# A gapless opening, and query and key projections in three products of rounded parts for images 3 to 7

## The chip, the core and the metric

The kernel runs on one core of a Trainium2 chip. The core has five engines that run their own instruction streams and meet only at semaphores: TensorE (PE in the rows, with its weight loads as PEld), VectorE (DVE), ScalarE (ACT), GpSimd (POOL) and SyncE (SP), which here issues all transfers. TensorE reads SBUF and writes PSUM; GpSimd works on SBUF alone. The metric is the device time of one launch in microseconds (us).

## What is computed

An attention block on eight images of 32 x 32 pixels with 64 channels, in float32: a group norm (8 groups), projections to queries, keys and values, a softmax over all 1024 pixels, the output projection, and the normalised input added back.

```
xf = group_norm(x, gamma, beta).reshape(B, N, C)      # B=8, N=1024, C=64
q, k, v = xf @ wq + bq, xf @ wk + bk, xf @ wv + bv
attn = softmax(einsum('bnc,bmc->bnm', q, k) * C ** -0.5)
out = einsum('bnm,bmc->bnc', attn, v) @ wp + bp
return xf + out
```

## The kernel before

**Tiles.** An image lies in SBUF twice: turned (`x_T`, channels in the partitions, pixels 0 to 511 in partitions 0 to 63 and 512 to 1023 in partitions 64 to 127) for the projections, and pixel by pixel (`values`) for the weighing and the residual. The scores of an image are made in eight tiles `i` of 128 x 1024, each exponentiated by ScalarE into `probs[i]` (L411); TensorE weighs the values with them (L846), and GpSimd adds the eight tiles up for the denominators (`sum_probs`, L309, seven additions per image).

**Number formats.** Matmuls in float32 are two instructions each in the trace. The scores are made of rounded parts instead: `q_hi`, `q_lo`, `k_hi`, `step_hi`, `step_lo` have the type fp32r, and each matmul with them is one instruction. A value is split by rounding it to fp32r (high part) and subtracting (low part); three products, high x high, high x low and low x high, stand in for the full one (`score_terms`, L788). The projections of queries (`project_q`, L752, two products that use one half of the rows each) and keys (`project_k`, L746, two products that use one half of the columns each) are in float32.

**Blocks.** A block `b` is the work in which the scores of image `b` are exponentiated and weighed. Image `p = b + 1` gets its row maxima in the same block (`max_chunk`, L759: eight chunks, each reduced by VectorE in L582 before the next may overwrite `wide`), image `s = b + 2` is normalised and projected, and image `z = b + 3` has its statistics taken. Normalising is one VectorE instruction (`normalise`, L537); the statistics go TensorE (mean) - ScalarE (squares) - TensorE (variance) - VectorE (`add_eps`, L529) - GpSimd (`rstd_of`, L275) - ScalarE (`gain_of`, L376). The block ends with the projection of image `s`, the transposed maxima, the weighing of tiles 6 and 7 and the output projection (L870). Images 0 and 1 are prepared by hand-written code in the opening. There the first chunks of maxima (L759, L582) follow the projection of image 0, and `keep_warm` (L876) issues products of ones that nobody reads.

**What sets the order.** Each engine's order is written out by hand; only semaphores tie them. In block 0 ScalarE waits for `gain_of(2)` between tiles 4 and 5. GpSimd's order in a block is the seven additions, then `rstd_of(z)`, `split_first(s)` (L291), `split_step(s)` (L296). TensorE's order at a block's end reads:

```
next_max_chunk(p, 7)
pe.wait_ge(xn_done, s - 1)
pe.wait_ge(exp_done, T * b + T)
project_q(s, ...)
project_k(s, ...)
```

## Time and profile before

| | us |
|---|---|
| median of 3 runs (200.02 to 200.08) | 200.05 |
| the profiled execution | 201.43 |
| its span, from first to last instruction | 199.6 |
| TensorE busy in the span | 189.2 |
| GpSimd busy | 143.4 |
| VectorE busy | 136.1 |
| ScalarE busy | 111.2 |

The profiled execution is 1.38 us longer than the median, and 1.83 us of it lie around the span. Times in rows are microseconds from the span's start. TensorE's matmuls are pipelined and overlap in the rows, so the start of one to the start of the next is the honest price.

### The profile page before, as it was taken

The numbers are of one execution on the slowest core, as the hardware profiler recorded it, in microseconds if no ns is written. First come the engines' busy times: TensorE is split into PE (matmuls) and PEld (weight loads), VectorE is DVE, ScalarE is ACT, GpSimd is POOL, SyncE is SP. The second block draws the span as 40 slices with busy tenths as digits, with TensorE's granted clock in tenths as the row PEclk, the third lists the DMA queues.
The fourth block names the chain that finished last, engine by engine and source line by source line (L and its number), as shares of the span: only waits on it lengthen the run. The fifth ranks groups of instructions, "written<-read, shape, count | busy, mean of one in ns | idle before, by whom it ended". The sixth has DMA issues, their size and how long they took to land.

```text
span 199.6 us, 3301 instructions
## 1 busy us (share of the span) xinstructions
PE 189.2 (95%) x1226; PEld 97.3 (49%) x1226; DVE 136.1 (68%) x179; ACT 111.2 (56%) x181; POOL 143.4 (72%) x92
## 2 busy tenths in 40 slices
PE   7895989989999999999999999999999999999993
PEld 7721435533564365536454466436452646444432
DVE  3239656697569786678767685868667856909763
ACT  2519267646865466546863676546544665338611
POOL 4108559599999979999699969996999869970000
PEclk9758599999999999999999999999999999999999
DMA  5594000000000001000100010000100010001002
GB/s 169 197 393 162 0 0 3 0 0 7 0 2 0 3 13 43 3 0 2 56 0 0 2 56 2 0 0 22 36 0 2 5 53 0 0 5 53 0 9 100
DMA packets 4415, 6.95 MB, mean 35 GB/s; under 512 B 832, under 2 KB 1456, under 8 KB 4400
## 3 DMA queue, kind: packets, MB, share of 16 engines
q1 hardware_dynamic: 4400, 6.75, 9.6%
q8 instruction: 10, 0.16, 0.4%
q14 instruction: 5, 0.04, 0.1%
HBM read 4.59 MB, written 2.10 MB: 34 GB/s over the span
## 4 chain that ended last, share of the span: by engine, by line
PE 80%; DVE 5%; DMA 4%; issue 3%; POOL 3%; ACT 2%; SPq 1%; DVEq 0%; POOLq 0%; ACTq 0%
PE attn L846 25%; PE scores L788 24%; PE wide L759 10%; PE scores L752 4%; PE misc L870 3%; PE scores L746 3%; DVE chunk_max L582 3%; POOL prob_sum L309 2%; DMA packed<-in_packed_dram 2%; PE misc L854 2%; PE attn L746 2%; DMA max_rows<-max_T 2%; PE misc L734 1%; ACT probs L411 1%; PE misc L861 1%
## 5 line engine op out<-in xcount | busy, mean ns | idle before, releaser
L309 POOL TENSOR_TENSOR prob_sum<-prob_sum,probs 128x1024 f32<-128x1024 f32 x42 | 102.0, 2428 | 5.7
L582 DVE TENSOR_REDUCE chunk_max<-wide 128x1 f32<-128x1024 f32 x60 | 73.4, 1223 | 31.5 <-PE wide L759 31.0
L411 ACT ACTIVATE probs<-scores 128x1024 f32<-128x1024 f32 x64 | 63.1, 1022 | 29.3 <-PE scores L788 28.5
L846 PE MATMUL attn<-probs,values 128*64 128x512 f32 x256 | 62.0, 605 | 0.0
L759 PE MATMUL wide<-k_hi,q_hi 64*128 64x512 f32 x120 | 31.0, 483 | 1.8 <-DVE chunk_max L582 1.8
L846 PEld LDWEIGHTS attn<-probs,values 128*64 128x64 f32 x256 | 15.6, 136 | 26.5 <-issue 24.1
L309 POOL TENSOR_TENSOR prob_sum<-probs 128x1024 f32<-128x1024 f32 x7 | 16.7, 2380 | 11.8 <-ACT probs L411 11.8
L759 PEld LDWEIGHTS wide<-k_hi,q_hi 64*128 64x128 f32 x120 | 12.5, 185 | 22.9 <-DVE chunk_max L582 13.2
L788 PE MATMUL scores<-q_hi,step_hi 64*128 64x512 f32 x96 | 20.7, 425 | 0.5
L788 PE MATMUL scores<-q_lo,step_hi 64*128 64x512 f32 x96 | 19.2, 391 | 0.0
L788 PE MATMUL scores<-q_hi,step_lo 64*128 64x512 f32 x96 | 19.1, 391 | 0.0
L383 ACT ACTIVATE q_hi<-scores,bias_q 128x512 fp32r<-128x512 f32 x13 | 8.9, 685 | 15.1 <-PE scores L752 15.1
L275 POOL TENSOR_TENSOR rstd<-var_eps,minus_half 128x1 f32<-128x1 f32 x8 | 4.4, 552 | 12.2 <-DVE var_eps L529 12.2
L788 PEld LDWEIGHTS scores<-q_hi,step_hi 64*128 64x128 f32 x96 | 9.2, 185 | 6.8 <-ACT probs L411 3.1
L788 PEld LDWEIGHTS scores<-q_lo,step_hi 64*128 64x128 f32 x96 | 9.2, 184 | 1.9
L599 DVE TENSOR_TENSOR misc<-misc,inv_den 128x512 f32<-128x512 f32 x7 | 4.9, 699 | 7.5 <-PE misc L870 7.5
L788 PEld LDWEIGHTS scores<-q_hi,step_lo 64*128 64x128 f32 x96 | 9.2, 185 | 1.4
L752 PE MATMUL scores<-xn,packed 64*128 64x512 f32 x28 | 8.3, 674 | 0.7 <-DVE xn L537 0.7
L567 DVE SCALAR_TENSOR_TENSOR q_lo<-scores,bias_q,q_hi 128x512 fp32r<-128x512 f32 x12 | 8.8, 729 | 0.0
L870 PEld LDWEIGHTS misc<-w_vp_s,attn_T 128*64 128x64 f32 x112 | 6.5, 137 | 3.8 <-issue 3.8
L296 POOL TENSOR_TENSOR step_lo<-step,step_hi 128x384 fp32r<-128x384 f32 x8 | 8.1, 1016 | 0.0
L620 DVE TENSOR_TENSOR prob_sum<-prob_sum,probs 128x1024 f32<-128x1024 f32 x6 | 7.3, 1218 | 1.1 <-ACT probs L411 0.6
(132 smaller groups left out, 236.7 us busy)
## 6 DMA issues: line engine op xcount, KB each, us to landing
x_T<-in_x_turned_dram SPq DMA_DIRECT2D x8, 256.0 KB, 6.4
values<-in_x_dram SPq DMA_DIRECT2D x8, 256.0 KB, 6.5
out_dram<-y_out SPq DMA_DIRECT2D x7, 256.0 KB, 2.0
out_dram<-y_out SPq DMA_DIRECT2D x2, 128.0 KB, 1.7
max_rows<-max_T SPq DMA_DIRECT2D x14, 4.0 KB
packed<-in_packed_dram SPq DMA_DIRECT2D x1, 192.0 KB, 4.5
packed<-in_packed_dram SPq DMA_DIRECT2D x1, 130.5 KB, 2.9
bp_all<-in_bp_dram SPq DMA_DIRECT2D x1, 32.0 KB, 4.1
```

What stands on the lines that cost most here:

```text
L296: nc.gpsimd.tensor_tensor(step_lo[s % RING][:, :], step[s % 2][:, :], step_hi[s % RING][:, :].bitcast(fp32), ALU.subtract).then_inc(step_l ...
L309: nc.gpsimd.tensor_tensor(prob_sum[b % 2][:, :], so_far[:, :], probs[i][:, :], ALU.add).then_inc(sum_done, 1)
L383: nc.scalar.activation(q_hi[s % RING][:, half], made_in, ACT.Identity, bias=bias_q[:, 0:1]).then_inc(q_hi_done, 1)
L411: nc.scalar.activation(probs[i][:, :], scores[flip_of(b, i)][:, :], ACT.Exp, scale=SCALE).then_inc(exp_done, 1)
L567: nc.vector.scalar_tensor_tensor(q_lo[s % RING][:, half], made_in, bias_q[:, 0:1], q_hi[s % RING][:, half].bitcast(fp32), ALU.add, ALU.sub ...
L582: nc.vector.reduce_max(chunk_max[:, p, j:j + 1], made_in[:, :], AX.X).then_inc(max_done, 1)
L746: product = nc.tensor.matmul(to[cols, :], wk2[:, cols], xn[s % 2][:, :], start=True, stop=True)
L752: product = nc.tensor.matmul(to[x_half], wq2[rows, :], xn[s % 2][rows, :], start=True, stop=True)
L759: product = nc.tensor.matmul(to[:, half], q_hi[p % RING][rows, chunk], k_hi[p % RING][rows, :], start=True, stop=True)
L788: product = nc.tensor.matmul(scores[flip][:, half], weights, queries[rows, half], start=(tt == 0 and term == 0), stop=(final and term == t ...
L846: product = nc.tensor.matmul(attn[x_half * C:(x_half + 1) * C, :], values[b][:, t * C:(t + 1) * C], probs[i][:, x_half * HALF:(x_half + 1) ...
L870: product = nc.tensor.matmul(misc[cols, tt * P:(tt + 1) * P], attn_T[b % 2][:, queries], w_vp_s[b % 2][:, :], start=True, stop=True)
```

## The change

It has four parts.

1. **Opening.** One more warm product ahead of the variance of image 0, and two more after the projection of image 0. The mean of image 0 is put in a row (`in_row`) before the weights are waited for instead of after the bias products. ScalarE's copy of `w_vp` waits for a semaphore of its own (`w_vp_made`) that comes after the first two products with the weights. VectorE rounds `k_hi[0]` ahead of `bias_out`.
2. **Image 2** is normalised by ScalarE in two steps (centre, then scale) instead of VectorE; tile 5 of block 0 is exponentiated ahead of `gain_of(2)`.
3. **Images 3 to 7** are projected in three products of rounded parts. VectorE normalises (now as a TENSOR_SCALAR), ScalarE rounds to `xn_hi`, VectorE subtracts to `xn_lo`. The weights are split once, in block 1: ScalarE rounds after tile 5, GpSimd subtracts ahead of its seventh addition.
4. **GpSimd's pause**: in blocks 1 to 5 its third addition waits for `xn_lo`.

The core of the diff, shortened:

```
@@ gpsimd, the loop over additions
                 for i in range(1, T):
+                    if b > 0 and exists(s) and i == 3:
+                        pool.wait_ge(xn_lo_done, s - 2)
+                    if b == 1 and i == 7:
+                        pool.wait_ge(weights_loaded, DMA)
+                        pool.wait_ge(w_hi_done, 2)
+                        for lo, weight, hi in ((wq_lo, wq2, wq_hi), (wk_lo, wk2, wk_hi)):
+                            nc.gpsimd.tensor_tensor(lo[:, :], weight, hi[:, :].bitcast(fp32),
+                                                    ALU.subtract).then_inc(w_lo_done, 1)
                     sum_probs(b, i)
@@ scalar
+            def round_xn(s):
+                act.wait_ge(xn_done, s - 2)
...
+                nc.scalar.copy(xn_hi[s % 2][:, :], xn[s % 2][:, :]).then_inc(xn_hi_done, 1)
-            act.wait_ge(biases_made, 1)
+            act.wait_ge(w_vp_made, 1)
...
                 exp_tile(b, 3)
+                if b > 0 and exists(s):
+                    round_xn(s)
...
+                if b == 1:
+                    nc.scalar.copy(wq_hi[:, :], wq2).then_inc(w_hi_done, 1)
+                    nc.scalar.copy(wk_hi[:, :], wk2).then_inc(w_hi_done, 1)
@@ vector
-                nc.vector.scalar_tensor_tensor(xn[s % 2][:, :], x_T[s][:, :], minus_mean[:, s:s + 1],
-                                               gain_col[:, s:s + 1].to_broadcast([P, HALF]), ALU.add,
-                                               ALU.mult).then_inc(xn_done, 1)
+                nc.vector.tensor_scalar(xn[s % 2][:, :], x_T[s][:, :], minus_mean[:, s:s + 1], gain_col[:, s:s + 1],
+                                        ALU.add, ALU.mult).then_inc(xn_done, 1)
+            def rest_of_xn(s):
+                dve.wait_ge(xn_hi_done, s - 2)
...
+                nc.vector.tensor_tensor(xn_lo[s % 2][:, :], xn[s % 2][:, :], xn_hi[s % 2][:, :].bitcast(fp32),
+                                        ALU.subtract).then_inc(xn_lo_done, 1)
@@ tensor
+                terms = ((wq_hi, wk_hi, xn_hi[u]), (wq_lo, wk_lo, xn_hi[u]), (wq_hi, wk_hi, xn_lo[u]))
...
+                    if s == 2:
+                        pe.wait_ge(third_xn_done, 1)
...
+                    else:
+                        pe.wait_ge(xn_lo_done, s - 2)
+                        pe.wait_ge(w_lo_done, 2)
+                        project_in_parts(s, (scores[1][:, 0:HALF], scores[1][:, HALF:PIXELS]), scores[0][:, 0:HALF])
```

**TensorE in the opening**, from the warm products ahead of the variance to the first maximum (L876 is `keep_warm`, L734 `in_row`, L895 and L896 the bias products, L746 and L752 the projection of image 0). Before:

```order
L876 MATMUL scores<-ones 128x128 x4
L729 MATMUL attn<-square_sum,packed 64x1 x2
L889 MATMUL wide<-packed 64x64 x2
...
L895 MATMUL wide<-w_vp,packed 128x64
L896 MATMUL wide<-packed 128x64
L734 MATMUL misc<-packed,minus_mean 128x64
L876 MATMUL scores<-ones 128x128
L746 MATMUL attn<-xn,packed 64x512 x2
L752 MATMUL scores<-xn,packed 128x512 x2
...
L759 MATMUL scores<-k_hi,q_hi 128x512 x2
```

And now, with the line numbers of the changed kernel (L941 is `keep_warm`, L785 `in_row`, L797 and L803 the projections, L824 the maxima):

```order
L941 MATMUL scores<-ones 128x128 x5
L780 MATMUL attn<-square_sum,packed 64x1 x2
L785 MATMUL misc<-packed,minus_mean 128x64
L956 MATMUL wide<-packed 64x64 x2
...
L963 MATMUL wide<-w_vp,packed 128x64
L964 MATMUL wide<-packed 128x64
L941 MATMUL scores<-ones 128x128
L797 MATMUL attn<-xn,packed 64x512 x2
L803 MATMUL scores<-xn,packed 128x512 x2
...
L941 MATMUL scores<-ones 128x128 x2
L824 MATMUL scores<-k_hi,q_hi 128x512 x2
```

The mean's row has moved ahead of the products with the weights, and two warm products stand between the projection and the first maximum.

**GpSimd in block 1**, from its last work of block 0 to its last of block 1. Before:

```order
L275 TENSOR_TENSOR rstd<-var_eps,minus_half 128x1
L291 TENSOR_TENSOR first_lo<-keys,k_hi 128x128
L296 TENSOR_TENSOR step_lo<-step,step_hi 128x384
L309 TENSOR_TENSOR prob_sum<-probs 128x1024
L309 TENSOR_TENSOR prob_sum<-prob_sum,probs 128x1024 x6
```

And now:

```order
L284 TENSOR_TENSOR rstd<-var_eps,minus_half 128x1
L300 TENSOR_TENSOR first_lo<-keys,k_hi 128x128
L305 TENSOR_TENSOR step_lo<-step,step_hi 128x384
L318 TENSOR_TENSOR prob_sum<-probs 128x1024
L318 TENSOR_TENSOR prob_sum<-prob_sum,probs 128x1024 x5
L352 TENSOR_TENSOR wq_lo<-packed,wq_hi 128x128
L352 TENSOR_TENSOR wk_lo<-packed,wk_hi 128x128
L318 TENSOR_TENSOR prob_sum<-prob_sum,probs 128x1024
```

The two subtractions for the weights stand behind the sixth of block 1's seven additions.

**TensorE at the end of block 1**, the projection of image 3. Before it is four products, each of two instructions when it runs:

```order
L759 MATMUL wide<-k_hi,q_hi 128x512 x2
L846 MATMUL attn<-probs,values 64x512 x4
L759 MATMUL wide<-k_hi,q_hi 128x512 x2
L752 MATMUL scores<-xn,packed 128x512 x2
L746 MATMUL scores<-xn,packed 64x512 x2
L729 MATMUL misc<-square_sum,packed 64x1 x2
```

And now:

```order
L824 MATMUL wide<-k_hi,q_hi 128x512 x2
L911 MATMUL attn<-probs,values 64x512 x4
L824 MATMUL wide<-k_hi,q_hi 128x512 x2
L812 MATMUL scores<-xn_hi,wq_hi 128x512 x2
L812 MATMUL scores<-xn_hi,wq_lo 128x512 x2
L812 MATMUL scores<-xn_lo,wq_hi 128x512 x2
L816 MATMUL scores<-xn_hi,wk_hi 128x512
L816 MATMUL scores<-xn_hi,wk_lo 128x512
L816 MATMUL scores<-xn_lo,wk_hi 128x512
L780 MATMUL misc<-square_sum,packed 64x1 x2
```

Nothing else on TensorE moves there; the first of these products now waits for `xn_lo` and for both weight remainders.

## Rows read from the trace of the kernel before

**Rows 1.** The page: busy time of each engine, and the chain's shares.
```profile
PE 189.2 (95%) x1226; PEld 97.3 (49%) x1226; DVE 136.1 (68%) x179; ACT 111.2 (56%) x181; POOL 143.4 (72%) x92
PE 80%; DVE 5%; DMA 4%; issue 3%; POOL 3%; ACT 2%; SPq 1%; DVEq 0%; POOLq 0%; ACTq 0%
```
**Rows 2.** A stretch (block 3): length, busy us (instructions) of PE, PEld, DVE, ACT, POOL, granted clock.
```profile
93.35:114.95 21.60, 21.55 (x153) 11.23 (x152) 15.74 (x21) 13.34 (x22) 18.98 (x11) 1.00 0.04 13
```
**Rows 3.** The same view of short stretches of the opening.
```profile
7.50:8.00 0.50, 0.31 (x5) 0.21 (x5) 0.44 (x1) 0.34 (x2) 0.00 (x0) 0.92 0.49 171
14.50:15.00 0.50, 0.34 (x5) 0.21 (x4) 0.16 (x1) 0.50 (x2) 0.10 (x1) 0.75 1.06 389
16.00:18.00 2.00, 0.77 (x4) 0.37 (x4) 2.00 (x3) 2.00 (x5) 1.58 (x3) 1.00 0.56 207
18.00:18.50 0.50, 0.23 (x2) 0.00 (x0) 0.50 (x1) 0.47 (x2) 0.50 (x1) 0.66 0.00 0
24.50:25.00 0.50, 0.50 (x4) 0.33 (x2) 0.18 (x1) 0.00 (x0) 0.24 (x1) 0.52 0.00 0
```
**Rows 4.** Chain of waits in the opening: start us, us, what.
```profile
8.13 0.69 PE wide L895 x2
8.81 0.43 PE wide L896 x2
9.24 0.43 PE misc L734 x2
9.67 0.72 PE scores L876 x2
10.39 1.91 PE attn L746 x4
12.30 2.03 PE scores L752 x4
```
**Rows 5.** Timeline, opening: start, us, engine, line, [idle before <-releaser].
```profile
7.53 0.20 PEld L723 LDWEIGHTS wide<-sum_T,packed 128*64 128x64 f32 x4
15.32 1.23 DVE L582 TENSOR_REDUCE chunk_max<-scores 128x1 f32<-128x1024 f32 x1 [0.50 <-PE scores L759]
23.46 1.22 DVE L582 TENSOR_REDUCE chunk_max<-scores 128x1 f32<-128x1024 f32 x1 [1.26 <-PE scores L759]
26.03 1.22 DVE L582 TENSOR_REDUCE chunk_max<-wide 128x1 f32<-128x1024 f32 x1 [1.35 <-PE wide L759]
```
**Rows 6.** Timeline, end of block 0 and projection of image 3 in block 1.
```profile
42.83 1.74 DVE L537 SCALAR_TENSOR_TENSOR xn<-x_T,minus_mean,gain_col 128x512 f32<-128x512 f32 x1
44.63 1.13 PE L752 MATMUL scores<-xn,packed 64*128 64x512 f32 x4 [0.68 <-DVE xn L537]
66.19 1.02 PE L752 MATMUL scores<-xn,packed 64*128 64x512 f32 x4
68.06 0.23 PE L729 MATMUL misc<-square_sum,packed 128*64 128x1 f32 x4
```
**Rows 7.** Timeline of GpSimd, blocks 0 and 1.
```profile
38.61 0.55 POOL L275 TENSOR_TENSOR rstd<-var_eps,minus_half 128x1 f32<-128x1 f32 x1 [2.49 <-DVE var_eps L529]
39.13 12.72 POOL L309 TENSOR_TENSOR prob_sum<-prob_sum,probs 128x1024 f32<-128x1024 f32 x5
...
56.23 15.23 POOL L309 TENSOR_TENSOR prob_sum<-prob_sum,probs 128x1024 f32<-128x1024 f32 x6
...
66.59 2.36 POOL L309 TENSOR_TENSOR prob_sum<-prob_sum,probs 128x1024 f32<-128x1024 f32 x1
71.93 0.46 POOL L291 TENSOR_TENSOR first_lo<-keys,k_hi 128x128 fp32r<-128x128 f32 x1
72.35 1.02 POOL L296 TENSOR_TENSOR step_lo<-step,step_hi 128x384 fp32r<-128x384 f32 x1
```
**Rows 8.** Chain of waits, a pair of score tiles in block 1: six pairs of fp32r products.
```profile
57.02 1.39 PE scores L788 x12
```
**Rows 9.** The page's groups: xcount | busy us, mean ns of one | idle before.
```profile
L788 PEld LDWEIGHTS scores<-q_hi,step_lo 64*128 64x128 f32 x96 | 9.2, 185 | 1.4
```

More of the change, by code:

```diff
@@ L86, in attention_block @@
         xn = [sb(f"xn{u}", [P, HALF]) for u in range(2)]
+        xn_hi = [sb(f"xn_hi{u}", [P, HALF], fp32r) for u in range(2)]
+        xn_lo = [sb(f"xn_lo{u}", [P, HALF], fp32r) for u in range(2)]
+        wq_hi, wq_lo, wk_hi, wk_lo = (sb(name, [P, P], fp32r) for name in ("wq_hi", "wq_lo", "wk_hi", "wk_lo"))
         q_first = sb("q_first", [P, PIXELS])
@@ L149, in attention_block @@
         second_xn_done = sem("second_xn_done")
+        third_xn_done = sem("third_xn_done")
         xn_done = sem("xn_done")
+        xn_hi_done = sem("xn_hi_done")
+        xn_lo_done = sem("xn_lo_done")
+        w_hi_done = sem("w_hi_done")
+        w_lo_done = sem("w_lo_done")
         first_mean_row_made = sem("first_mean_row_made")
@@ L502, in _ @@
                     sum_squares(z)
+                exp_tile(b, 5)
                 if b == 0:
+                    act.wait_ge(mean_done, 1)
+                    act.wait_ge(centred_T_done, 1)
+                    act.wait_ge(second_xn_done, 1)
+                    nc.scalar.activation(centred_T[:, :], x_T[2][:, :], ACT.Identity,
+                                         bias=minus_mean[:, 2:3]).then_inc(centred_T_done, 1)
                     gain_of(s)
[L505 removed]
                 if 0 < b < LAST:
                     scale_w_vp(b - 1)
+                if b == 1:
+                    nc.scalar.copy(wq_hi[:, :], wq2).then_inc(w_hi_done, 1)
+                    nc.scalar.copy(wk_hi[:, :], wk2).then_inc(w_hi_done, 1)
                 exp_tile(b, 6)
+                if b == 0:
+                    act.wait_ge(centred_T_done, 2)
+                    act.wait_ge(gain_done, 2)
+                    act.wait_ge(q_made, 1)
+                    act.wait_ge(k_made, 1)
+                    nc.scalar.activation(xn[0][:, :], centred_T[:, :], ACT.Identity,
+                                         scale=gain_col[:, 2:3]).then_inc(third_xn_done, 1)
                 exp_tile(b, 7)
@@ L671, in _ @@
                 reduce_chunk(p, 3, wide)
+                if b > 0 and exists(s):
+                    rest_of_xn(s)
                 reduce_chunk(p, 4, wide)
@@ L753, in project_q, with project_in_parts @@
                 product.then_inc(q_made, 1)
+            def project_in_parts(s, to_q, to_k):
+                u = s % 2
+                terms = ((wq_hi, wk_hi, xn_hi[u]), (wq_lo, wk_lo, xn_hi[u]), (wq_hi, wk_hi, xn_lo[u]))
+                for n, (weight, _, normed) in enumerate(terms):
+                    for x_half in range(2):
+                        rows = slice(x_half * C, (x_half + 1) * C)
+                        product = nc.tensor.matmul(to_q[x_half], weight[rows, :], normed[rows, :], start=(n == 0),
+                                                   stop=(n == 2), skip_group_check=True)
+                product.then_inc(q_made, 1)
+                for n, (_, weight, normed) in enumerate(terms):
+                    product = nc.tensor.matmul(to_k, weight[:, :], normed[:, :], start=(n == 0), stop=(n == 2),
+                                               skip_group_check=True)
+                product.then_inc(k_made, 1)
             def max_chunk(p, j, to):
@@ L883, in _ @@
             group_mean(0, attn[:, 0:1])
-            keep_warm(scores[1], 4)
+            keep_warm(scores[1], 5)
             pe.wait_ge(squares_done, 1)
             group_variance(0, attn[:, 1:2])
+            pe.wait_ge(first_mean_done, 1)
+            in_row(minus_mean[0:C, 0:1], misc[:, MEAN_ROW]).then_inc(first_mean_row_made, 1)
             pe.wait_ge(weights_loaded, DMA)
             for rows in column_halves():
-                nc.tensor.matmul(wide[rows, 0:C], w_v_turned, w_p, start=True, stop=True)
+                product = nc.tensor.matmul(wide[rows, 0:C], w_v_turned, w_p, start=True, stop=True)
+            product.then_inc(w_vp_made, 1)
             nc.tensor.matmul(wide[:, HALF:HALF + 1], wq2[0:C, :], beta_col[0:C, :], start=True, stop=True)
```

30 lines of the change are left out of this document (18 added, 12 removed).

## The prediction

> **What bounds the kernel now.** I read the page first: TensorE is busy for 189.2 of 199.6 us, and the chain that ended last runs through it for 80% [rows 1]. A busy TensorE need not be a full one, so the blocks were read one by one next: block 3 lasts 21.60 us with TensorE busy for 21.55 at the full clock, GpSimd for 18.98, VectorE for 15.74, ScalarE for 13.34 [rows 2]. In the blocks TensorE is the bound, and GpSimd is the only engine near it. What is removed from TensorE's stream there comes off the time, as long as GpSimd's 19 us still fit. The third view is the granted clock in the opening: it falls to half within 7.50 to 8.00 (mean 0.92), is back within 14.50 to 15.00, falls again within 18.00 to 18.50 after a stretch in which TensorE was busy for 0.77 of 2 us, and is back near 25.0 [rows 3]. So two stretches of 6.8 us run at 1.2 GHz, and the chain there is TensorE's until the first maxima [rows 4]. The fourth view is GpSimd's timeline from block 0 to block 1 [rows 7].
>
> **The opening, first part.** Between 8.13 and 14.33 the chain is six groups of TensorE, all at half clock [rows 4]. The row of the mean (L734, 0.43) leaves it: it now runs while the weights are still on their way. ScalarE copies `w_vp` after the first two products with the weights instead of after all four, so L895 can follow L723, which ends at 7.73 [rows 5], instead of 8.13: 0.35 off after a semaphore. What is left of L895, L896 and L876 is 1.84 us at half clock, 0.92 at full. L746 and L752 took 1.91 and 2.03; later, at full clock, the two take 1.87 from 66.19 to 68.06 [rows 6], so 2.07 comes off. Sum if the clock holds: 0.43 + 0.35 + 0.92 + 2.07 = 3.8. A warm product (two instructions) took 0.72 at half clock [rows 4], 0.36 at full. The two new ones behind the projection take 0.72, of which more than half passes while TensorE has to wait for `q_hi` anyway; 0.3 is paid. The extra product ahead of the variance fills a wait for the squares and the weights and only brushes the path. I take **3.5 us**.
>
> Does the clock hold? Just before its fall TensorE is busy for 0.31 of 0.50 us [rows 3], with one-column and 64-column products and waits for `w_vp`. The change puts 0.36 us of full-array products and the mean's row into the stretch before the fall and lets L895 start sooner. These rows do not price the gate; they say that the work in that stretch grows and its gaps shrink, so I hold it for likely. If it does not hold, 0.43 + 0.35 = 0.8 stays, less what the two warm products cost.
>
> **The opening, second part.** The first reduction starts at 15.32, and the eighth at 26.03, after VectorE stood idle for 1.26 and 1.35 us before the last two because TensorE was slow [rows 5]. With the first part done 3.5 us sooner, TensorE still waits for reductions of 1.22 us each between chunks, as in 16.00 to 18.00 (0.77 of 2 us busy [rows 3]), and the clock should fall again, only sooner. Then the second part just shifts: nothing more is won. If it does not fall, VectorE's idle 2.6 us go, less some 0.7 (an estimate: the projection of image 1 and the first score products still stand between those chunks); 1.9 more.
>
> **Image 2 and block 0.** TensorE waits in block 0 for VectorE's `xn` (L537, 42.83 to 44.57) and starts the projection at 44.63 [rows 6]. ScalarE makes it sooner now, and the last exponential, chunk 7 and the projection can start near 43.6: 1.0 us less in block 0. By the next step this is lost again.
>
> **Image 3, and the weight remainders.** GpSimd subtracts them behind its sixth addition of block 1. That addition ran from 66.59 to 68.95 [rows 7], and it cannot come sooner: from `rstd` of image 2 at 38.61 on, five additions fill 39.13 to 51.85, the next `rstd`, two splits and the first addition of block 1 follow, and six additions fill 56.23 to 71.46, none with idle time before it; and that first `rstd` waits 2.49 us for VectorE, which hangs on TensorE's block 0 [rows 7]. Two 128 x 128 subtractions of the kind of L291 start 0.42 apart and take 0.46 [rows 7]: 0.88 us, so the weights are ready at 69.85. TensorE wants them at 66.19 [rows 6], and with block 0 shortened at 65.2. **It waits 4.7 us.** A late `xn_lo` in the same block could push GpSimd back by some tenths; I set it to nothing, since in block 0 VectorE's L537, which took 1.74 us beside GpSimd's additions [rows 6], is gone. In parts, the projection is three pairs for the queries and three full products for the keys. Pairs of fp32r products follow one another in 1.39 / 6 = 0.232 us [rows 8]; six steps are 1.39 against 1.87. L729 then comes at 69.9 + 1.4 = 71.3 instead of 68.06 [rows 6]: **3.2 us lost**, all savings of blocks 0 and 1 counted.
>
> **The clock after that wait.** 4.7 idle us are more than TensorE had before either fall in rows 3. After the second fall full work was needed until 25.0. At half clock each us costs half: between 0 (it holds) and 6.8 / 2 = 3.4 (as long as the stretches of rows 3, all of it after the wait). Part of the low stretch should fall into the wait itself, so I take the lower half of that range, **1.5 us**.
>
> **Images 4 to 7.** 1.87 - 1.39 = 0.48 each, with everything behind at its pace: **1.9 us** won. The bounds are 0 (below) and 0.55. The added work is covered: neither ScalarE's rounding nor VectorE's subtraction should be longer than L537's 1.74 us [rows 6], and ScalarE has 8.3 us idle per block, VectorE 5.9 [rows 2]. GpSimd's third addition waits for `xn_lo`, at least for nothing and at most for a reduction (1.22 [rows 5]) and a subtraction of half its columns, 1.9 us together; I take 1. Its block has 21.60 - 18.98 = 2.6 us to spare [rows 2], the shorter block takes 0.5 of them, so 1.1 us of cover stay with my value and 0.2 with the worst. If it were gone, the denominators (and TensorE behind them) would come late by what is missing in each block.
>
> A rule speaks against this part. The pair of rows 8 uses the same half of the rows in one pair after the other and still steps at 0.232 us with its weight loads included. The Trainium skill, TensorE: Matmul & The Clock Gate, section on packing small matmuls, says that a weight load overlaps matmuls in flight only where the row group differs; by it the three full-array key products would each show their load. The trace doesn't agree for the halves, and has no run of full-array fp32r products.
>
> **Sum.** -3.5 (opening) + 3.2 (wait in block 1) + 1.5 (clock after it) - 1.9 (images 4 to 7) = -0.7 us. The profiled execution, 201.43, would come to 200.7; from the median of 200.05 it is 199.3. The terms are differences of chains, and 1.4 us between the two executions changes none of them by more than 0.03.
>
> **Rivals.**
> (a) The clock also holds through the reductions: 1.9 more, -2.6, **197.4**. For it: the two warm products come just ahead of them. Against it: between reductions the rows show TensorE busy for 0.77 of 2 us.
> (b) The clock falls at 7.9 as before: the opening gives 0.8 instead of 3.5, the sum is +2.0, **202.0**: slower. It decides from an opening gain of less than 2.8 us on, since 3.2 + 1.5 - 1.9 = 2.8 has to be paid for.
> (c) The clock after the wait costs the full 3.4: +1.2, **201.2**.
> (d) Full-array weight loads are not hidden: loads of 64 x 128 take 0.19 us each [rows 9], three per image on five images are +2.85 by that: +2.1, **202.2**. This is what the rule of the Trainium skill named above would bring.
> (e) The wait in block 1 isn't there, because GpSimd comes sooner than its rows say: -3.5 - 1.0 - 5 x 0.48 = -6.9, **193.1**. Against it stands an unbroken row of GpSimd instructions over 31 us.
>
> **Chances.** The forecast 0.44, with a range of its own of 198.3 to 200.3 from the bounds of the opening (3 to 4) and of the clock (0.8 to 2.2); (a) 0.22; (b) 0.13; (c) 0.09; (d) 0.05; (e) 0.07. A measurement of this kernel can tell about 0.2%, 0.4 us, from no change. Of the forecast's 0.44, 0.31 lie beyond -0.4, 0.11 within, 0.02 above. With (a) and (e) faster has 0.60; same takes 0.03 from (c): 0.14; the rest of (c), (b) and (d) is slower: 0.26. The range from 197.0 to 202.1 leaves out (e), the lower end of (a) and the upper ends of (b) and (d).
>
> **What would show it.** Right: clock 1.00 from 4.5 through 11 us, first reduction near 11.9, `rstd` of image 2 near 35.1, TensorE idle for 4 to 5 us in block 1 until both weight remainders are made, half clock behind it, 1.4 us from the first product of a projection to the variance. Wrong: half clock at 8 us (b); the first fall missing altogether (a); less than 3 us idle in block 1 (e); key products more than 0.3 us apart (d); over 5 us of half clock after the wait (c).

## The result: slower by 2.8%

| | before | after |
|---|---|---|
| median, us | 200.06 (200.02 to 200.82) | 205.99 (205.49 to 206.17) |
| profiled execution, us | 201.43 | 206.17 |
| its span, mean granted clock | 199.6, 0.965 | 204.3, 0.958 |

The ratio is 1.028, with a 95% interval of 1.025 to 1.031. The forecast was 199.3 with a range from 197.0 to 202.1: wrong in sign and outside the range. Medians, here and below, count every execution; ratios leave out those that lie over 1.5% above the fastest of their kernel.

The page of the changed kernel, to be held against [rows 1]: busy times, shares of the chain that ended last, and TensorE's granted clock in 40 slices of 5.1 us.

```profile
PE 191.2 (94%) x1237; PEld 100.9 (49%) x1237; DVE 138.1 (68%) x183; ACT 115.8 (57%) x190; POOL 143.1 (70%) x94
PEclk9966699999999669999999999999999999999999
PE 82%; DVE 7%; POOL 5%; DMA 2%; issue 2%; SPq 1%; ACT 0%; DVEq 0%; POOLq 0%; ACTq 0%
```

GpSimd has 5% of the chain, and the clock row has a hole at slices 14 and 15 (68 to 75 us) that a kernel busy all the time should not have. **Where the 4.7 us of span came from** is read from one marker, the first maxima product behind each block's output projection. In the chains of both kernels its starts are:

| end of block | before | after | difference |
|---|---|---|---|
| 1 | 71.34 | 76.86 | +5.52 |
| 2 | 92.92 | 98.33 | +5.41 |
| 3 | 114.52 | 119.77 | +5.25 |
| 4 | 136.11 | 141.22 | +5.11 |
| 5 | 157.60 | 162.41 | +4.81 |
| end of span | 199.6 | 204.3 | +4.7 |

So everything is lost before 77 us, and the later blocks give 0.8 back, blocks 2 to 4 taking 21.44 to 21.47 us now instead of 21.58 to 21.60, and block 5 21.19 instead of 21.49. Block 3 as in [rows 2]:

```profile
98.33:119.77 21.44, 21.39 (x153) 11.57 (x153) 16.13 (x21) 13.98 (x23) 18.80 (x11) 1.00 0.04 13
```

**The opening.** Stretches in the form of [rows 3], and the chain in the form of [rows 4] (L941 is the warm product, L797 and L803 the projection of image 0):

```profile
6.80:10.20 3.40, 3.40 (x30) 2.76 (x31) 1.06 (x6) 1.24 (x5) 0.88 (x2) 1.00 0.74 274
10.20:13.60 3.40, 3.40 (x10) 0.63 (x8) 1.48 (x3) 0.00 (x1) 0.00 (x0) 0.50 1.05 396
...
17.10:20.40 3.30, 2.39 (x8) 0.97 (x10) 3.30 (x4) 2.19 (x5) 3.30 (x5) 0.50 0.11 41
20.50:23.80 3.30, 3.30 (x12) 1.39 (x14) 2.04 (x3) 1.30 (x2) 1.23 (x4) 0.50 0.00 0
```

```profile
5.14 2.12 PE scores L941 x10
...
9.94 1.60 PE attn L797 x4
11.54 2.01 PE scores L803 x4
```

The clock did not hold. It stood at full in the view until 10.2 and was half from there to 13.6, through nearly all of the projection of image 0. Then it fell again in the reductions. The start was slower too: the five warm products of 5.14 (ten instructions) took 2.12 us, 0.21 per instruction, where the execution of the opening alone (below) took 0.13. The clock view can't settle why, since it reads 1.00 from 0.7 us on in both. The pace looks like a clock that rose later, which is inferred and not shown. The first reduction starts at 14.93 instead of 15.32, and `rstd` of image 2 is made at 37.88 instead of 38.61 [rows 5, 7]: 0.73 us gained.

```profile
14.93 1.23 DVE L633 TENSOR_REDUCE chunk_max<-scores 128x1 f32<-128x1024 f32 x1 [0.90 <-PE scores L824]
...
37.88 0.55 POOL L284 TENSOR_TENSOR rstd<-var_eps,minus_half 128x1 f32<-128x1 f32 x1 [2.49 <-DVE var_eps L570]
```

**Block 1.** The timeline of GpSimd and VectorE (start, us, engine, line), then of TensorE, with one stretch of the clock view in between. To be held against [rows 6, 7].

```profile
55.24 2.38 POOL L318 TENSOR_TENSOR prob_sum<-prob_sum,probs 128x1024 f32<-128x1024 f32 x1
58.25 9.89 POOL L318 TENSOR_TENSOR prob_sum<-prob_sum,probs 128x1024 f32<-128x1024 f32 x4 [0.63 <-DVE xn_lo L589]
68.10 0.45 POOL L352 TENSOR_TENSOR wq_lo<-packed,wq_hi 128x128 fp32r<-128x128 f32 x1
68.51 0.45 POOL L352 TENSOR_TENSOR wk_lo<-packed,wk_hi 128x128 fp32r<-128x128 f32 x1
...
53.38 2.00 DVE L581 TENSOR_SCALAR xn<-x_T,minus_mean,gain_col 128x512 f32<-128x512 f32 x1
56.44 1.73 DVE L589 TENSOR_TENSOR xn_lo<-xn,xn_hi 128x512 fp32r<-128x512 f32 x1
```

```profile
68.30:75.00 6.70, 5.89 (x21) 2.79 (x23) 1.73 (x5) 2.63 (x5) 3.98 (x5) 0.50 0.02 4
```

```profile
69.11 0.79 PE L812 MATMUL scores<-xn_hi,wq_hi 64*128 64x512 f32 x2 [4.46 <-POOL wk_lo L352]
...
72.26 0.38 PE L780 MATMUL misc<-square_sum,packed 128*64 128x1 f32 x4
```

TensorE stands idle for 4.46 us until GpSimd's second subtraction is done. The clock goes to half at 68.25, 0.9 us before TensorE may run again, and stays there for 6.8 us. From the first product of the projection to the marker it takes 76.86 - 69.11 = 7.75 us; before it was 71.34 - 66.19 = 5.15.

**A projection in parts at full clock** (block 2). Each row starts a pair or a product; the second fence has two rows of the weight loads.

```profile
93.31 0.39 PE L812 MATMUL scores<-xn_hi,wq_hi 64*128 64x512 f32 x2
93.54 0.40 PE L812 MATMUL scores<-xn_hi,wq_lo 64*128 64x512 f32 x2
93.77 0.40 PE L812 MATMUL scores<-xn_lo,wq_hi 64*128 64x512 f32 x2
94.10 0.50 PE L816 MATMUL scores<-xn_hi,wk_hi 128*128 128x512 f32 x1
94.43 0.39 PE L816 MATMUL scores<-xn_hi,wk_lo 128*128 128x512 f32 x1
94.66 0.40 PE L816 MATMUL scores<-xn_lo,wk_hi 128*128 128x512 f32 x1
94.99 0.28 PE L780 MATMUL misc<-square_sum,packed 128*64 128x1 f32 x4
```

```profile
93.55 0.19 PEld L812 LDWEIGHTS scores<-xn_lo,wq_hi 64*128 64x128 f32 x2
94.09 0.19 PEld L816 LDWEIGHTS scores<-xn_hi,wk_hi 128*128 128x128 f32 x1 [0.36 <-issue]
```

The steps are 0.23, 0.23, 0.33, 0.33, 0.23, 0.33: 1.68 us instead of 1.39. Against 1.86 before, a projection gains 0.18, close to the 0.16 by which the block became shorter (21.60 to 21.44). The load for the third query pair starts at 93.55, 0.22 ahead of its products; the load for the first key product starts at 94.09, with its product, after PEld stood idle for 0.36.

### The profile page after: what moved, and what is told of

Its sections match the earlier page's. It is cut to its first block, busy times and chain, and to the rows that moved or that the text cites. A ratio compares the mean times of both kernels' runs of the same rounds, so it can differ in the third digit from the quotient of the medians.

```text
span 204.3 us, 3343 instructions
## 1 busy us (share of the span) xinstructions
PE 191.2 (94%) x1237; PEld 100.9 (49%) x1237; DVE 138.1 (68%) x183; ACT 115.8 (57%) x190; POOL 143.1 (70%) x94
## 4 chain that ended last, share of the span: by engine, by line
PE 82%; DVE 7%; POOL 5%; DMA 2%; issue 2%; SPq 1%; ACT 0%; DVEq 0%; POOLq 0%; ACTq 0%
PE attn L911 25%; PE scores L853 23%; PE wide L824 10%; POOL prob_sum L318 5%; DVE chunk_max L633 4%; PE scores L941 3%; PE misc L935 3%; PE scores L816 3%; PE scores L812 2%; DMA max_rows<-max_T 2%; PE attn L797 2%; PE misc L919 2%; PE scores L803 1%; PE misc L785 1%; PE misc L839 1%
## 5 line engine op out<-in xcount | busy, mean ns | idle before, releaser
L318 POOL TENSOR_TENSOR prob_sum<-prob_sum,probs 128x1024 f32<-128x1024 f32 x42 | 100.7, 2399 | 9.0 <-DVE xn_lo L589 4.2
L911 PE MATMUL attn<-probs,values 128*64 128x512 f32 x256 | 62.9, 613 | 0.0
L824 PE MATMUL wide<-k_hi,q_hi 64*128 64x512 f32 x120 | 31.1, 486 | 1.8 <-DVE chunk_max L633 1.8
L824 PEld LDWEIGHTS wide<-k_hi,q_hi 64*128 64x128 f32 x120 | 12.5, 187 | 22.9 <-DVE chunk_max L633 14.3
L570 DVE TENSOR_SCALAR var_eps<-misc 128x1 f32<-128x1 f32 x6 | 0.9, 157 | 11.3 <-PE misc L839 11.3
L941 PE MATMUL scores<-ones 128*128 128x128 f32 x32 | 7.2, 398 | 1.1 <-DVE ones L674 1.1
```

Of the source, the lines that this page charges most:

```text
L318: nc.gpsimd.tensor_tensor(prob_sum[b % 2][:, :], so_far[:, :], probs[i][:, :], ALU.add).then_inc(sum_done, 1)
L824: product = nc.tensor.matmul(to[:, half], q_hi[p % RING][rows, chunk], k_hi[p % RING][rows, :], start=True, stop=True)
L911: product = nc.tensor.matmul(attn[x_half * C:(x_half + 1) * C, :], values[b][:, t * C:(t + 1) * C], probs[i][:, x_half * HALF:(x_half + 1) ...
L941: nc.tensor.matmul(to[:, 0:P], ones[:, :], ones[:, :], start=True, stop=True)
```

## The experiments

An execution's clock has to be read first. Executions of one kernel differ in where the half-clock stretches of the opening lie: the kernel before, in 84 executions beside these runs, had spans of 199.2 to 199.7 us at a mean clock of 0.957, 199.0 at 0.964, 197.5 to 198.8 at 0.972, and 195.8 at 0.981 (and one of 287.3 at 0.564, left out here). So medians are given with their ratio to the kernel before on the same chip, and spans are compared at a like clock. That is a rough tool: the profiled execution of before had 199.6 at 0.965, and one kernel below had 199.3 and 200.9, both at 0.982. Differences under 1 us that are read this way alone are hints.

### The wait alone, on the kernel before

```
 GpSimd, block 1, before the seventh addition:
+    for lo, weight, hi in ((wq_lo, wq2, wq_hi), (wk_lo, wk2, wk_hi)):
+        tensor_tensor(lo, weight, hi, ALU.subtract).then_inc(w_lo_done, 1)
 ScalarE, block 1, before exp_tile(1, 6):
+    copy(wq_hi, wq2); copy(wk_hi, wk2)
 TensorE, before the float32 projection of image 3:
+    pe.wait_ge(w_lo_done, 2)
```

> The kernel before, with the wait alone: ScalarE rounds the two weights in block 1, GpSimd subtracts the rest behind its sixth addition of that block, and TensorE waits for both before it projects image 3. The projections stay float32 and nothing reads the remainders. Theory W (the wait and the half clock behind it are what the change loses): the remainders are made near 69.7, 3.5 us after the start of the projection at 66.19 in the trace of before; half clock behind the wait adds 2.5 to 3.4; no later block gives anything back. The kernel comes 5.5 to 7 us above the kernel before at a like clock elsewhere, near 206. Rival C (the clock behind the wait costs only the 1.5 us of the prediction, the rest of the loss came from the products in parts): near 205 or less, with the next block's first chunk 5 us behind that of before. Rival D (the wait in the change was made by the additions and by xn_lo, not by the place of the two subtractions): under 3 us of wait, near 203.

Median 207.52 (205.77 to 208.50), ratio 1.034 (1.027 to 1.042): above the 206 that I had expected, with two of the four executions at a mean clock of 0.941. The profiled execution has a span of 205.2, 5.6 above the profiled one of before, though its opening was 0.96 quicker. Its chain:

```profile
65.40 3.50 issue
68.89 2.08 PE scores L764 x4
70.97 1.90 PE scores L758 x4
```

Measured from the maxima product ahead of the projection, the projection starts 4.00 us later (64.89, 68.89) where it stood 0.34 behind (65.85, 66.19): 3.66 of wait. Projection to marker takes 77.02 - 68.89 = 8.13, 3.0 more than before. The wait and the clock behind it make 6.6 us, more than the whole difference of the change. Theory W holds. Rival D falls, since here there are no products in parts, no `xn_lo` and no pause, and the wait is there all the same. Rival C (1.5 us for the clock) falls with the 3.0.

### The same wait, with TensorE kept busy in it

```
 TensorE, the changed kernel, before the projection of image 3:
+    keep_warm(scores[1], 18)
```

> The changed kernel with 18 warm products of ones that TensorE issues while it waits for the weight remainders in block 1 (some 4.5 us of work, into the tile that the projection then overwrites). The wait stays, only the engine is not idle. If the 6 us at half clock behind the wait come from the idleness: clock 1.00 there, 2.5 to 3 us less than the changed kernel, 203 to 203.5. If the clock falls anyway: 206.

Median 203.01 (201.16 to 204.25), ratio 1.011 (1.005 to 1.017): 3 us below the changed kernel, although TensorE starts no sooner. Clock view of the profiled execution, the longest of the four (span 202.5), and the two ends:

```profile
60.00:74.90 14.90, 14.65 (x107) 9.02 (x103) 8.75 (x14) 5.64 (x10) 13.02 (x10) 1.00 0.01 2
...
69.77 0.50 PE L812 MATMUL scores<-xn_hi,wq_hi 64*128 64x512 f32 x2 [0.25 <-POOL wk_lo L352]
...
74.83 0.51 PE L824 MATMUL wide<-k_hi,q_hi 64*128 64x512 f32 x2
```

The clock stays at 1.00, and the marker comes 5.06 us behind the projection, in the changed kernel 7.69 by the same view (76.80). So the clock behind the wait cost 2.6 us.

### The wait taken away: weights split in the opening

```
 ScalarE, opening, behind sum_squares(1):
+    copy(wq_hi, wq2); copy(wk_hi, wk2)
 GpSimd, opening, behind rstd_of(1):
+    both subtractions
 (both removed from block 1)
```

> The changed kernel, but ScalarE rounds the weights and GpSimd subtracts them in the opening, where both stand idle, so that TensorE finds the remainders ready in block 1. Everything else stays. Theory W (the loss is the wait for the weight remainders in block 1 and the half clock behind it): the idle stretch of 4.9 us and the 6 us at half clock go, 6 to 7.5 us less than the changed kernel, 198.5 to 200, or less if block 0's shortening now counts. Rival P (the loss lies in the rounding work, the pause or the products in parts of every block): at most 1 us less, 205 to 206.

Median 199.24 (198.09 to 200.12), ratio 0.997 (0.993 to 1.002): 6.7 us below the changed kernel. The subtractions lie at 14.23 and 14.64 us, where GpSimd has time, and the projection of image 3 follows the maxima at 63.43 directly:

```profile
63.77 0.39 PE L811 MATMUL scores<-xn_hi,wq_hi 64*128 64x512 f32 x2
...
65.44 0.28 PE L779 MATMUL misc<-square_sum,packed 128*64 128x1 f32 x4
```

At a mean clock of 0.957 its span is 198.3, against 199.5 before: 1.2 us for image 2 (below) and the projections in parts together. Rival P falls: nothing that stays in every block made the loss.

### Without GpSimd's pause

```
 GpSimd, before the third addition (in the kernel just above):
-    pool.wait_ge(xn_lo_done, s - 2)
```

> The kernel with the weight remainders made in the opening, without GpSimd's wait for xn_lo ahead of its third addition. If the pause is covered and so is VectorE's work (theory): the same time within 0.5 us at a like clock, GpSimd without its idle 0.9 us per block, xn_lo starting only when the third addition has ended and ready 1.5 to 2.5 us later than with the pause, still ahead of TensorE's projection. Rival (xn_lo then comes behind the projection's start, since VectorE is held for one or two additions of 2.4 us and its reductions with it): TensorE idle 0.5 to 1.5 us per block, 3 to 7 us slower in all.

Median 198.89 (196.10 to 200.25), ratio 0.990 (0.984 to 0.996); at a like clock it agrees with the kernel with the pause in most executions (198.3 to 198.5 at 0.957, 197.1 at 0.974), but two had spans of 194.3 and 194.7 at 0.982, where that kernel had 196.3 at 0.983; no trace shows why. In its block 2 the subtraction fell right among the additions and was not held up:

```profile
97.99 2.60 POOL L318 TENSOR_TENSOR prob_sum<-prob_sum,probs 128x1024 f32<-128x1024 f32 x1
...
100.73 2.92 POOL L318 TENSOR_TENSOR prob_sum<-prob_sum,probs 128x1024 f32<-128x1024 f32 x1
...
100.74 0.68 DVE L586 TENSOR_TENSOR xn_lo<-xn,xn_hi 128x512 fp32r<-128x512 f32 x1
```

The pause cost nothing, as forecast, but it bought nothing either. I had expected `xn_lo` to come 1.5 to 2.5 us later; it takes its 0.68 us inside the row of additions, beside the one of 100.73, which takes 2.92 instead of some 2.4. Here it is GpSimd that gives way, and it has the time: the six additions of this block take 15.73 us, with the pause 2.61 and 12.47. In block 1 `xn` and `xn_lo` took 2.02 and 1.73, with or without the pause.

### The order of the products

```
 project_in_parts (weights split early): the three key products ahead of the three query pairs
```

> The kernel with the weight remainders made in the opening, with the three full-array key products ahead of the three pairs of query products. Theory (about 0.1 us of weight load shows at each passage between half-row pairs and full-array products, and at each full-array product behind another): the projection stays at 1.6 to 1.75 us from its first product to the variance, with steps of 0.33 for the keys and 0.23 within the query pairs; the kernel's time is the same within 0.4 us. Rival (the 0.1 us belongs to the change of PSUM bank or the place in the block, not to the array shape): the first three steps, now keys, take 0.23 each, and the query pairs behind them the longer ones. The query maxima's inputs come later by 0.7 us, which should cost nothing, since the ScalarE and VectorE work behind them has spare time.

Median 200.04 (198.05 to 201.18), ratio 0.995 (0.991 to 1.000). Projection of image 3:

```profile
63.88 0.50 PE L809 MATMUL scores<-xn_hi,wk_hi 128*128 128x512 f32 x1
64.22 0.40 PE L809 MATMUL scores<-xn_hi,wk_lo 128*128 128x512 f32 x1
64.45 0.39 PE L809 MATMUL scores<-xn_lo,wk_hi 128*128 128x512 f32 x1
64.77 0.50 PE L815 MATMUL scores<-xn_hi,wq_hi 64*128 64x512 f32 x2
65.11 0.39 PE L815 MATMUL scores<-xn_hi,wq_lo 64*128 64x512 f32 x2
```

Steps of 0.34, 0.23, 0.32, 0.34 in these rows, and 0.23 to the third pair (65.34). A full-array product behind another steps at 0.23 like the halves; the 0.1 us sits on both sides of a passage from half the rows to all of them, or back. With the keys first there is one more passage ahead of them (the maxima use halves): the maxima product just before takes 0.43 instead of 0.34, and the projection 1.78 instead of 1.67 with the queries first. The theory holds in its first half and not in its second (a product behind its like shows no load). I had expected the same time within 0.4 us, and that was missed: blocks 2 to 4 take 21.65 to 21.67 us instead of 21.43 to 21.45, and at a like clock the spans lie about 1 us higher (199.2 to 199.4 against 198.3 at 0.957). The Trainium skill, TensorE: Matmul & The Clock Gate, section on packing small matmuls, has it that a weight load overlaps matmuls in flight only where the row group differs. The load that starts only with the first key product (94.09 above) agrees with that; the 0.23 of a full-array product behind another does not. That the 0.1 us is a load is inferred from these rows and not tested apart.

### The parts of the change, one by one

The opening alone, on the kernel before:

> The kernel before with only the first part of the change, the opening. The trace of the changed kernel has rstd of image 2 at 37.88 instead of 38.61 us, 0.7 us sooner, where I forecast 3.5. If 0.7 is what the opening is worth: 199.3. If that one trace was an unlucky position of the clock's low stretches: down to 197.

Median 199.26 (197.67 to 200.68), ratio 0.988 (0.983 to 0.993). Two executions had spans of 196.0 at 0.980, two 198.9 at 0.972. The profiled one is of the first pair, and shows what I had forecast for the change:

```profile
4.65 1.31 PE scores L877 x10
...
3.90:14.10 10.20, 8.82 (x65) 5.77 (x63) 5.04 (x14) 6.00 (x16) 2.71 (x5) 1.00 0.78 274
14.20:20.90 6.70, 5.78 (x18) 2.47 (x20) 5.44 (x6) 3.55 (x7) 4.70 (x9) 0.50 0.46 168
...
34.98 0.55 POOL L276 TENSOR_TENSOR rstd<-var_eps,minus_half 128x1 f32<-128x1 f32 x1 [2.52 <-DVE var_eps L530]
```

`rstd` at 34.98 is 3.6 us sooner than in [rows 7]; the term of 3.5 is what this opening gives when the clock holds. But the kernel before itself had an execution with a span of 195.8 at 0.981. So the opening shows no worth of its own here, apart from how often the clock holds, which four executions can't tell.

Image 2 on ScalarE alone, on the kernel before:

> The kernel before with the third image normalised by ScalarE in block 0 instead of VectorE. As forecast for the change: TensorE no longer waits for VectorE's product of block 0 (1.74 us long there), the projection of image 2 starts 0.9 to 1.0 us sooner, and without the later wait of block 1 this stays: 0.9 to 1.0 us below the kernel before at a like clock, near 199.5. Rival (the next thing in block 0, GpSimd's sums or the last exponential, is late instead): 0 to 0.4 us.

Median 199.74 (196.72 to 200.28), ratio 0.989 (0.985 to 0.993); 198.1 to 198.4 at 0.957 against 199.3 to 199.7. The forecast of 1.0 us holds. The opening and image 2 together, with float32 projections:

> The kernel before with the opening and image 2 normalised by ScalarE, projections of all images in float32 and no pause. By W and by the chain of block 0: 0.7 from the opening and 1.0 from block 0, 198.3. Beside e1 it shows what the products in parts are worth without the wait: by the periods of 21.45 against 21.60 us, 0.15 us each, 0.7 us in all; by my forecast 2.4.

Median 198.63 (197.50 to 200.41), ratio 0.993 (0.988 to 0.997); 198.6 at 0.966. The kernel with the weights split early has 197.8 to 198.1 there, so its projections in parts are worth 0.5 to 0.8 us on five images; at 0.974 it is 0.2 to 0.7 (197.4 against 196.7 to 197.2), and at 0.983 about 0.4 (196.7 or 196.8 in three of four executions against 196.3). Per image this is at most 0.16. The blocks say it more exactly: 21.57 to 21.59 us with float32 projections and 21.43 to 21.45 in parts, 0.14 each. That is near the 0.18 of the rows above and far from 0.48.

The changed kernel with the old opening:

> The changed kernel with the opening of before: mean's row behind the products with the weights, four warm products, none behind the projection of image 1, VectorE's order of before. Theory O (the new opening gave only the 0.7 us that its profile shows, because the half clock sits elsewhere): 0.5 to 1 us above the changed kernel at a like mean clock, 206.5 to 207.2. Rival P (the opening is worth the 3.5 of the prediction and something else in the changed kernel lost 3 us more): near 209. Rival Q (the new opening shifts the low stretches for the worse): at or under 205.5.

Median 205.84 (205.18 to 206.85), ratio 1.027 (1.022 to 1.033): the changed kernel's time, and 0.7 below the least that theory O had expected. Rival P falls. The profiled execution reached `rstd` of image 2 at 38.62, 0.74 later than the changed kernel, and the weight remainders with it; but behind the wait it took 6.44 us to the marker (69.85 to 76.29) instead of 7.69. The half-clock stretch there is 3.4 us long instead of 6.8, from 69.66 to 73.07. The early weights with the old opening:

> The kernel with the weight remainders made in the opening, with the order of the opening as before (mean's row behind the products with the weights, four warm products, none behind the projection of image 1). Theory O (the new opening is worth only the 0.43 + 0.35 us of its chain, and whether the clock holds in it varies from execution to execution): 0.5 to 1 us above the same kernel with the new opening at a like mean clock; the clocks themselves spread over the same levels, 0.957 to 0.983. Rival P (it is worth 3.5): near 202. Rival Q (it is worth nothing): the same.

Median 198.79 (198.23 to 199.72), ratio 0.991 (0.988 to 0.995). At 0.957 the span is 197.5, at 0.974 196.4 to 196.9; with the new opening, on another chip, 198.3 and 196.7 to 197.2. At a like clock the new order shows no gain, in these runs rather a loss of about 0.5 us: theory O's 0.5 to 1 us for the chain alone is not seen either.

### What holds the clock in the opening

```
 TensorE, opening, between the first maxima products:
+    keep_warm(misc, 1)    behind max_chunk(0, 1)
+    keep_warm(misc, 2)    behind each of max_chunk(0, 2), (0, 3), (0, 4)
+    keep_warm(misc, 1)    behind max_chunk(0, 5)
```

With early weights and the new opening:

> The kernel with the weight remainders made in the opening, plus eight warm products of TensorE in the gaps between the first maxima products, where TensorE waits 0.5 to 1.1 us each for a reduction (in its profile the clock was half from 9.2 to 12.6 and from 19.5 to 23.0 there). Theory G (both the half-clock stretches of the opening come from TensorE's thin work before them; what the opening gives is decided by the clock and by nothing of the chain): the second half-clock stretch is gone, the chain before the eighth reduction is 0.8 to 1.5 us shorter, the mean clock is 0.98 or above in nearly all executions, the scatter between executions shrinks, and the median is near 197.5 to 198. Rival (the clock falls there whatever TensorE does): same clock and times as without the warm products, or up to 1 us longer where a warm product (0.72 us at half clock) holds up the next maxima product.

Median 196.89 (194.72 to 197.43), ratio 0.980 (0.975 to 0.984): the fastest version here, 9 us below the changed kernel. The clock row has one dip left, and two warm products in a gap (four instructions) take 0.71 us:

```profile
PEclk9979999999999999999999999999999999999998
...
17.32 0.71 PE L940 MATMUL misc<-ones 128*128 128x128 f32 x4
...
14.00:23.00 9.00, 8.24 (x47) 4.64 (x46) 8.11 (x7) 6.21 (x13) 7.25 (x14) 1.00 0.39 142
```

All six executions had a mean clock of 0.987 to 0.998. The same on another chip, without the pause:

> Early weight remainders, new order of the opening, eight warm products between the first maxima, and no pause of GpSimd. Theory: the same as with the pause, mean clock 0.987, span near 195, median 196.9, ratio to the kernel before 0.975 to 0.984 in every execution. Rival (the six even executions with the pause were luck of one chip, since the old order with the same warm products spread from 196.4 to 202.5 us on another): two groups again, near 196.5 and at 199 to 202.

Median 197.19, ratio 0.988 (0.984 to 0.992). Ten of twelve executions had 0.986 to 0.991 and spans of 194.9 to 196.0; the other two 0.969 with 197.7, and 0.945 with 201.3. So it was no luck of one chip, but it isn't every execution either.

The same warm products with the old opening, and on the kernel before:

> The kernel with early weight remainders and the old order of the opening, plus the same eight warm products between the first maxima. Theory G (what an opening gives is decided by the clock in it; the new order itself is worth at most its 0.8 us of chain): mean clock 0.98 or above in nearly all executions as with the new order, and the time within 0 to 0.8 us above that of the new order with the warm products (ratio to the kernel before 0.98 to 0.984). Rival H (the new order is what keeps the clock up in the first part, and the warm products do so only in the second): one 6.8 us stretch at half clock more, mean clock 0.97, 1.5 us or more above, ratio 0.987 to 0.99. Rival I (the old order is the better one, as the runs without warm products hint): ratio under 0.979.

> The kernel before with nothing but the eight warm products between the first maxima. Theory G: the half-clock stretch that lies in the reductions goes, mean clock 0.98 or above, about 1.5 to 3 us below the kernel before (ratio 0.985 to 0.992), with less scatter. Rival (the first half-clock stretch, of the part ahead of the maxima, only grows or stays twice as long in the old order): mean clock 0.97 as in its better executions, under 1 us.

Two groups each. Old opening: spans of 194.6 and 194.8 at 0.988, and four of 199.3 to 200.7 at 0.945 to 0.962. Kernel before: four of 196.3 to 197.0 at 0.991, and three of 201.0 to 202.5 at 0.949 to 0.966. Medians 201.19 and 198.84, ratios 0.980 (0.976 to 0.985) and 0.990 (0.986 to 0.994). In the first kernel's profiled execution, with a span of 199.3, the clock is at 0.50 from 17 to 22 us all the same, and there the warm products are in the way:

```profile
17.72 1.22 PE L940 MATMUL misc<-ones 128*128 128x128 f32 x4
18.87 0.79 PE L823 MATMUL scores<-k_hi,q_hi 64*128 64x512 f32 x2
```

From the start of two warm products to the start of the next two (17.72 to 19.60) it is 1.88 us, more than a reduction's 1.22, so TensorE leads the chain. No expectation fits both groups: the quick one meets theory G's 0.98, and the other is longer than rival H has it. What H says of the order comes nearest: with the new order the warm products kept the clock up in 20 of 23 executions (those of the last kernel below among them), with the old one in 6 of 13. That suggests that the new order helps, and not why. It is not shown: the old order with warm products ran on one chip alone, the new one on two others.

Last, the changed kernel with nothing but these warm products:

> The changed kernel with nothing but the eight warm products between the first maxima. Theory G2 (new order and warm products together keep the clock up in the opening; the wait in block 1 is untouched): one half-clock stretch of 3.4 us in the opening instead of 10.2, mean clock 0.97 with the one behind the wait, the next block's first chunk 3 to 4 us sooner than in the changed kernel, 202 to 203, ratio to the kernel before 1.008 to 1.016. Rival (in this kernel the clock falls all the same, and warm products at half clock cost 1.22 us a pair): 206 to 208.

Median 203.01, four of five executions within 203.00 to 203.29 at 0.981, one at 210.04; ratio 1.017 (1.011 to 1.024). 3.0 us below the changed kernel, and the wait is there unchanged. TensorE may run again 1.95 us sooner (67.16 for 69.11), and 1.2 more are won behind the wait:

```profile
35.92 0.55 POOL L284 TENSOR_TENSOR rstd<-var_eps,minus_half 128x1 f32<-128x1 f32 x1 [2.50 <-DVE var_eps L570]
...
67.16 0.76 PE L812 MATMUL scores<-xn_hi,wq_hi 64*128 64x512 f32 x2 [4.47 <-POOL wk_lo L352]
...
67.30:70.60 3.30, 3.30 (x14) 1.85 (x15) 0.00 (x0) 0.90 (x2) 2.04 (x1) 0.50 0.00 0
...
73.66 0.50 PE L824 MATMUL wide<-k_hi,q_hi 64*128 64x512 f32 x2
```

Here only 3.4 us are at half clock, all of them behind the wait, and projection to marker takes 6.50.

## Why the prediction was wrong

Between the profiled executions the forecast was -0.7 us and +4.7 came: 5.4 too low, in three terms.

1. **The opening: forecast -3.5, measured -0.73.** The step that failed is "Does the clock hold?". I read the busy share just ahead of the fall at 7.9 and held it for likely that more work there lets the clock stand. It did stand at 7.9; instead the start was 0.8 slower (2.12 us against 1.31 for the five warm products), and the clock fell at 10.2, behind 3.4 us in which TensorE was busy throughout, and was half through the projection. The trace of one execution could not show that these stretches move from one execution to the next. A term that hangs on the place of such a stretch should have been carried at both of its values. Rival (b) has 0.8 for the opening, near the measured 0.73, but that is luck in part: it has the fall at 7.9 and 6.8 us long, and here it came at 10.2 and was 3.4 us long, with the slower start on top. A small misreading stands beside it: 7.73 is the end of a weight load (rows 5), and its products run to 7.81, so the 0.35 was nearer 0.3.
2. **The wait in block 1: forecast 3.66 us late at the start of the projection, measured 3.65** (69.11 - 66.19 + 0.73). GpSimd took 31.09 us from `rstd` of image 2 to the second remainder, 31.24 by the rows of before; the idle time was 4.46 for a forecast 4.7. Reading an engine's unbroken row of work through two blocks was right. That it fits to 0.01 is luck: VectorE's `xn` and `xn_lo` each took over a us longer than in later blocks and made GpSimd wait 0.63, a term set to nothing in the prediction, and shorter additions made it up (five in block 0 12.43 us instead of 12.67, five in block 1 12.23 instead of 12.72).
3. **The clock behind it: forecast 1.5, measured 2.6** in the changed kernel (7.69 against 5.06 with warm products in the wait), 3.0 in the wait alone, 1.4 where only 3.4 us of half clock lay behind (6.50 against 5.06). The step that failed is "Part of the low stretch should fall into the wait itself": only 0.9 of 6.8 us did, 0.7 in the wait alone and nothing in the changed kernel with warm products in the opening. The bounds of 0 to 3.4 held; rival (c), which takes the upper end, was the nearest for this term.
4. **Images 4 to 7: forecast -1.9, measured -0.8.** The step that failed is "six steps are 1.39". The rate of 0.232 us of [rows 8] was carried to a sequence that changes between halves and full rows; three of its six steps take 0.33. Rival (d) had the right place and the wrong size: 0.1 at three steps, not 0.19 at three products, and no part of it between like products. The same 0.3 us is missing in image 3's projection, at full clock.
5. **Right:** image 2 (1.0), and the pause and the added work of ScalarE and VectorE, which the blocks cover. The kernel with no wait, rival (e), was put 6.2 us below the forecast, and the kernel with the weights split early came 6.7 below the changed one. This fits only in part by its terms: the clock was 1.1 dearer than forecast and image 3's projection 0.3 less of a gain.

Added up: 2.8 (opening) + 1.6 (projection to marker: 7.75 - 5.15 = 2.6 for the forecast 1.5 - 0.5) + 1.1 (images 4 to 7) = 5.5, the 5.4 missed but for rounding. The sum went to the wrong side at the first term alone: with 0.73 it is +2.1, near rival (b)'s 202.0; the other two made it 206. The chances treated opening and clock behind the wait as cases that exclude one another. Both ask whether the clock stays up, which the rows of one execution did not answer, and both fell to the same side.

## What to carry to other kernels

A remainder that is needed once belongs where its engine is idle, not in the block that first needs it: the same two subtractions of 0.45 us cost 6.6 us in block 1 and no wait of TensorE in the opening. A wait of 4.5 us on TensorE costs its length and up to 3 us more at half clock behind it, and filling it with products into a free bank saves the second part though not the first. Before pricing a clock stretch, look at several executions' mean clock: where they differ for one kernel, take the gain as unproven and see whether filling the gaps makes the executions agree.

## What was not expected of the hardware

- The place of the half-clock stretches is not a property of the kernel: the unchanged kernel had spans from 195.8 to 199.7 us with mean granted clocks from 0.981 to 0.956, leaving out the one of 287.3. The clock can be half under fully busy TensorE, as from 10.2 to 13.6 in the changed kernel (3.40 of 3.40 us busy).
- VectorE's instructions that read two tensors, or one in float32, from SBUF took 0.54 (`xn`) and 0.68 (`xn_lo`) in block 2, but 2.00 and 1.73 in block 1, where they start in the middle of one of GpSimd's additions and end 0.3 to 0.6 us behind it (53.38 + 2.00 = 55.38 behind the one up to 55.10; 56.44 + 1.73 = 58.17 behind the one up to 57.62). Yet in block 2 without the pause `xn_lo` took 0.68 beside an addition, and the addition 2.92. The Trainium skill, GPSIMD Engine Reference, section Key points, names two SBUF inputs and the two-port modes as what contends with GpSimd; the rows show VectorE held in one block and GpSimd in another. In the rows shown it goes by the start: the instructions that start 0.65 and 1.20 us into an addition are not done before it ends, and the `xn_lo` of 100.74, which starts with its addition (100.73), is not held but slows it. No experiment moved the starts on purpose, so that this decides it is a reading and not shown.
- Warm products are two-edged: two of them took 0.71 us at full clock and fit the gap, at half clock they took 1.22 and do not. In most of the executions where the clock fell all the same the kernel came 4 to 7 us behind its quick ones (201.0 to 202.5 against 196.3 to 197.0; 208.3 against 201.2).
